# A recurrent block with a routed feed-forward beside it: the f2 stage of an item moved into the following step

## The reference

```
xn = layernorm(x)
for l in 0..3:                                    # branch 1, each item apart
    k, q, v = split(h @ Wkqv[l])
    r = tril(q k^T)/sqrt(128) / (1 + sqrt(row));  r = r / clip(|row sum|, 1);  u = r v
    a, g = split(u @ Wm1 + bm1);  m = a * silu(g) @ Wm2 + bm2
    y = groupnorm1(m) + h                         # mean and variance over the whole item
    f = gelu(y @ Wf1 + bf1) @ Wf2 + bf2
    h = layernorm(f + y) * ln_g + ln_b
e = argmax(softmax(xn @ gate_w))                  # branch 2, one of 8 experts a token
t = prob_e * (gelu(xn @ w1[e] + b1[e]) @ w2[e] + b2[e])
out = x + h * silu(t)
```

## Time and profile before

| | |
|---|---|
| median of 3 runs | 515.69 us (514.87 to 517.4) |
| the profiled execution, its own time | 514.47 us |
| its span, first to last instruction | 512.4 us |
| PE, DVE, ACT, POOL busy | 93%, 75%, 50%, 49% |
| granted TensorE clock, mean | 0.97 |

### The profile page before, as it was taken

The page is one execution under the profiler, slowest core; times in us unless marked ns, Lnnn a source line. Parts: engine busy times, 40 slices in busy tenths (PEclk is TensorE's granted clock), DMA queues, the critical chain, the costliest instruction groups (busy, mean ns, idle before and its releaser), DMA issues.

```text
span 512.4 us, 9849 instructions
## 1 busy us (share of the span) xinstructions
PE 475.0 (93%) x3147; PEld 395.4 (77%) x3147; DVE 384.8 (75%) x1348; ACT 253.7 (50%) x533; POOL 252.5 (49%) x279
## 2 busy tenths in 40 slices
PE   6999889999999999999999999999999999997472
PEld 5887666667888988898889888988888888675242
DVE  4768888878777786677777866777778777888766
ACT  4822434444566655555666555556665544453420
POOL 4520288887545445554454455544444555333341
PEclk9998999999999999999999999999999999999856
DMA  9999411112511111110111111201111000500202
GB/s 265 232 122 222 156 37 38 37 33 78 103 64 58 42 58 42 59 63 32 59 57 44 58 51 48 65 31 59 62 51 46 10 12 12 164 1 1 61 19 84
DMA packets 47345, 35.05 MB, mean 68 GB/s; under 512 B 13320, under 2 KB 38736, under 8 KB 47296
## 3 DMA queue, kind: packets, MB, share of 16 engines
q1 hardware_dynamic: 44496, 28.94, 22.1%
q0 software_dynamic: 2272, 4.71, 2.7%
q10 hardware_dynamic: 528, 0.79, 0.5%
HBM read 14.70 MB, written 9.42 MB: 47 GB/s over the span
## 4 chain that ended last, share of the span: by engine, by line
PE 67%; DVE 12%; POOL 10%; issue 6%; DMA 2%; ACT 2%; POOLq 0%; SPq 0%; DVEq 0%; ACTq 0%
PE bank L1221 9%; PE bank L1148 7%; PE bank L1132 7%; POOL x_slots L471 5%; PE pair L1290 4%; PE pair L1266 4%; PE bank L1303 4%; PE bank L1159 4%; PE pair L1248 4%; PE bank L1160 4%; PE bank L1161 3%; PE pair L1292 3%; PE pair L1246 3%; PE bank L1203 2%; PE bank L1219 2%
## 5 line engine op out<-in xcount | busy, mean ns | idle before, releaser
L483 POOL TENSOR_TENSOR zhat<-zhat,all_lg 128x512 f32<-128x512 f32 x31 | 43.9, 1418 | 88.1 <-PE bank L1193 74.2
L1221 PE MATMUL bank<-all_f,G_sb 128*128 128x128 f32 x512 | 76.8, 284 | 0.0
L651 ACT ACTIVATE y_sb<-bank,gn_bi,gn_sc 128x512 f32<-128x512 f32 x32 | 24.9, 778 | 104.3 <-DVE gn_bi L993 104.2
L1221 PEld LDWEIGHTS bank<-all_f,G_sb 128*128 128x128 f32 x512 | 70.9, 201 | 1.4 <-issue 1.4
L646 ACT ACTIVATE uT_h<-bank 128x512 fp32r<-128x512 f32 x32 | 19.1, 597 | 100.8 <-PE bank L1203 100.8
L426 POOL TENSOR_TENSOR ln_rs<-ln_ve,half_neg 128x4 f32<-128x4 f32 x32 | 33.1, 1033 | 42.0 <-DVE ln_ve L675 41.7
L1132 PEld LDWEIGHTS bank<-moe_w,h_T 128*128 128x128 f32 x312 | 39.5, 191 | 13.9 <-issue 13.9
L498 POOL TENSOR_TENSOR gn_rs<-gn_ve,half_neg 128x1 f32<-128x1 f32 x32 | 18.5, 577 | 58.5 <-DVE gn_ve L888 58.4
L563 ACT ACTIVATE h_T<-bank,w_t 128x128 f32<-128x128 f32 x156 | 44.5, 372 | 5.1 <-PE bank L1148 5.1
L518 POOL DMA_INDIRECT y_rows<-yt,slot_info x39 | 40.9, 1048 | 11.0 <-POOL yt L515 11.0
L631 ACT ACTIVATE G_sb<-bank,all_par 128x512 f32<-128x512 f32 x64 | 43.1, 694 | 5.2 <-PE bank L1184 2.8
(11 more groups left out here) (177 smaller groups left out, 1233.8 us busy)
## 6 DMA issues: line engine op xcount, KB each, us to landing
w_t<-moe_w SPq DMA_DIRECT2D x39, 258.0 KB, 2.4
x_slots<-moe_w SPq DMA_DIRECT2D x1, 2515.5 KB, 20.4
xt<-x_slots SPq DMA_DIRECT2D x39, 64.0 KB, 1.8
x_sb<-in_L_attn_x SPq DMA_DIRECT2D x8, 256.0 KB, 5.7
moe_w<-in_L_ffn_w SPq DMA_DIRECT2D x1, 2048.0 KB, 20.0
moe_w<-y_rows SPq DMA_DIRECT2D x8, 256.0 KB, 4.6
out<-moe_w SPq DMA_DIRECT2D x7, 256.0 KB, 2.4
all_f<-in_L_attn_Wf SPq DMA_DIRECT2D x2, 512.0 KB, 4.2
```

The costliest lines, as they stand in the source:

```text
L483: pool.tensor_tensor(zhat[:, b % 2, :, :], zhat[:, b % 2, :, :], all_lg[:, li, :].unsqueeze(1).broadcast_to([P, C, D]), ALU.mult)\
L1221: last = mm(bank[7][:, at_c], G_sb[:, k, at_c], all_f2[:, li, k, :], start=False, stop=k == 1)
```

## The change

**What moves.** z and its statistics, the moments, the power, ln_nb and zhat of an item leave stage 2 and become the front of stage 3 of the following step. On PE z stands right behind q; the transposition of zhat goes to the rear, ahead of u's transposition and `means`. POOL's two htok instructions wait for zhat and write htok directly, no longer in place. The groupnorm affine and y (DVE, ACT) leave the rear of a step for the front of the next. y_sb has two buffers, since z reads y one step later. On DVE the causal mask goes behind the two products on gg_sb. On POOL `ln_pow` goes behind the first place of scatters, htok behind the second, and gn's power behind htok and the LATE tile's rows. In step 7 three f1 splits stand ahead of gn's power (before: two ahead, one behind). All 24 steps of layers 1 to 3 are parted. tanh, silu and outputs come later and in other portions.

**GpSimd in the routed steps of layer 0**, before, from one item's htok (steps 4 and 5): x_slots rows are scatters, gn_rs and ln_rs the two powers.

The core of the diff:

```diff
-        y_sb = sb("y_sb", [P, S])
+        y_sb = sb("y_sb", [P, 2, S])
         def parted(l, t):
-            return turn(l, t, EARLY) is not None and l > 0
+            return 0 < l < L
-        TANH_AT = {LB - 2: (0, 1, 2), LB - 1: (3, 4, 5), LB: (6, 7)}
-        SILU_AT = {LB - 2: (0, 1, 2), LB - 1: (3, 4, 5), LB: (6, 7)}
-        OUT_AT = {LB - 1: (0, 1, 2), LB: (3,), LB + 1: (4, 5)}
+        TANH_AT = {LB - 2: (0, 1), LB - 1: (2, 3), LB: (4, 5), LB + 1: (6, 7)}
+        SILU_AT = {LB - 2: (0, 1), LB - 1: (2, 3), LB: (4, 5), LB + 1: (6, 7)}
+        OUT_AT = {LB - 1: (0,), LB: (1, 2), LB + 1: (3, 4, 5)}
@@ gpsimd step
+                scatter(l, t, 0)
+                if w := at(l, t, 3, B, LB):
+                    ln_pow(w[0], w[1])
+                tile_rows(l, t, EARLY)
+                scatter(l, t, 1)
                 w = at(l, t, 3, B, LB)
...
-                    if n < LAST_LAYER:
-                        pool.wait_ge(pe_zT, n + 1)
-                    else:
-                        pool.wait_ge(z_done, n + 1)
-                    pool.tensor_tensor(zhat[:, b % 2, :, :], zhat[:, b % 2, :, :],
+                    pool.wait_ge(z_done, n + 1)
+                    pool.tensor_tensor(rows_b, zhat[:, b % 2, :, :],
...
                 tile_rows(l, t, LATE)
                 if w := at(l, t, 1, B, LB):
                     pool.wait_ge(gn_var, w[0] + 1)
...
-                scatter(l, t, 1)
-                if w := at(l, t, 2, B, LB):
-                    ln_pow(w[0], w[1])
@@ scalar step
+                tile_gelu(late_turn_before(l, t))
+                if w := at(l, t, 2, B, LB):
+                    n = w[0]
+                    act.wait_ge(gn_affine, n + 1)
+                    act.activation(y_sb[:, n % 2, :], bank[6][:, :], ACT.Identity, bias=gn_bi[:, :],
+                                   scale=gn_sc[:, :]).then_inc(gn_done, 1)
+                queries(l, t)
...
+                gate(l, t)
...
+                layernorm(l, t)
                 tile_gelu(turn(l, t, EARLY))
@@ tensor step
+                gelu_second(l, t)
...
-                if not first:
-                    tile_front(l, t, EARLY, n2 * 2)
-                if parted(l, t):
-                    zhat_by_feature(l, t)
+                tile_front(l, t, EARLY, n2 * 2)
...
-                for stage in ((gelu_second, means, u_by_feature) if first and 2 <= t < B - 1 else
-                              (means, gelu_second) if l == L else (u_by_feature, gelu_second, means)):
-                    stage(l, t)
+                zhat_by_feature(l, t)
+                u_by_feature(l, t)
+                means(l, t)
```

More of the change, by code:

```diff
@@ L589, in late_turn_before @@
             def late_turn_before(l, t):
[L591 removed]
+                if l * B + t == 0:
                     return None
@@ L930, in step @@
                                              ALU.add, ALU.mult).then_inc(act_done, 1)
+                if w := at(l, t, 0, B, LB):
+                    n, b, _ = w
+                    dve.wait_ge(pe_A, n + 1)
+                    dve.tensor_tensor(A_sb[:, :, :], pair[:, 0, :].rearrange("p (c i) -> p c i", c=C),
+                                      causal[:, :].unsqueeze(1).broadcast_to([P, C, P]), ALU.mult)\
+                        .then_inc(A_done, 1)
+                tile_in(l, t, EARLY)
+                if s == LB + 2:
+                    outputs((LAST_B - 1,))
+                if w := at(l, t, 3, B, LB):
+                    n, b, _ = w
+                    ln_shifts(n, b)
+                    need(dve, htok_done, n - 1)
+                    dve.wait_ge(ln_shift, n + 1)
+                    for c in range(C // 2):
+                        last = dve.tensor_scalar(zhat[:, b % 2, c, :], bank[7][:, c * D:(c + 1) * D],
+                                                 ln_rs[:, b % 2, c:c + 1], ln_nb[:, b % 2, c:c + 1], ALU.mult, ALU.add)
+                    last.then_inc(z_half, 1)
+                if s == LB + 2:
+                    finish_last()
                 if first and t == 1:
```

152 lines of the change are left out of this document (49 added, 103 removed).

## The result

The changed kernel takes 561.9 us (560.4 to 564.1, 4 runs) against 515.3 for the kernel before (513.4 to 517.4, 4 runs): ratio 1.091, 95% interval 1.085 to 1.097. The direction was forecast, the size was not: 543 us, range 526 to 555. The profiled execution has a span of 559.1 us against 512.4.

A forecast was written before the change was run, and what follows sets the result against it. TensorE was taken to set the pace from step 8 to 28, GpSimd in layer 0's routed steps. Terms 7.1 + 4.7 + 1.5 + 2.9 + 6.3 + 5.1 + 0.9 - 1 = 27.5 raised 514.5 to 542, median 543 us; range 526 to 555.

The forecast's parts named there:

- two-turn steps: Sixteen steps with two expert tiles (9 to 14, 16 to 21, 23 to 26): 15.25 us against 14.80, 7.0 us in all.
- some 0.2: Two-turn steps: TensorE's idle time, once ahead of f1's second half and once ahead of `means`.
- The round was closed through GpSimd alone: Two-turn steps: gs to gn_sc runs through the LATE yt, GpSimd's weighing, indirect DMA and gn's power, 3.13 us.
- One-turn steps: Steps 8, 15 and 22, with one expert tile: 14.73 us against 13.17, 4.7 us in all.
- The collision with htok: VectorE's gs with two SBUF inputs waits beside GpSimd's htok: 0.6 us more in a one-turn step.
- f1 in parts: f1 in three parts saves TensorE some 0.3 us in six steps where it isn't last: counted as nothing.
- Layer 0: Routed steps: steps 4 to 6 at 15.3 us against 13.27, 6.3 us in all; steps 1 to 3 add 5.1.
- Six scatters: Layer 0: they stand between gn's power and ln_rs on GpSimd, 7.7 us with the gap, while VectorE stands still.
- steps 1 to 3: Start of layer 0: a later mask, and step 2's power at some 64.2 instead of 60.6; 5.1 us.
- Steps 28 to 30: Step 28, same chain as one-turn steps with an EARLY yt: 1.5 us; tile-less steps 29 and 30: 2.6 together.
- The end: Step 32 onward: VectorE's queue adds up to 39.5 to 41 us against 40.98, so -1 us (-3.5 to 0.5).
- the second (557 us): Rival, 14%: two-turn steps collide too, as ln_rs stops gg or htok reaches gs; 0.8 x 17 = 14 us.

The follow-up runs named there:

- e1_loads: Changed kernel with TensorE's two register loads moved to the rear of the step before, ahead of zhat's transposition: 552.3 us, ratio 1.072.
- e11_double: Kernel before the change with TensorE's two register loads at the start of each step made twice: 532.1 us, ratio 1.031.
- e14_behind4: Kernel before the change with TensorE's register loads made twice and placed behind the Wm2 product: 525.8 us, ratio 1.019.
- e9_ahead: Changed kernel with VectorE's xtT of the EARLY tile ahead of the mask and TensorE's register loads right behind the Wm2 product: 544.5 us, ratio 1.053.
- e5_xtT: As e1_loads on the changed kernel, with VectorE's copy xtT of the EARLY tile also put ahead of the mask: 552.0 us, ratio 1.068.
- e4_gs: Changed kernel with gs's last two instructions as tensor_scalar with one tensor input instead of two in SBUF: 559.6 us, ratio 1.087.
- e8_f1: Kernel before the change with only f1 split in three parts in every step of layers 1 to 3: 526.5 us, ratio 1.018.
- e10_f1: Changed kernel with f1 in parts only in steps with an EARLY tile, as before the change: 560.0 us, ratio 1.082.
- e6_both: Changed kernel with four scatters instead of six ahead of ln_rs in layer 0, and gs without two SBUF inputs: 554.0 us, ratio 1.070.

## Why the prediction was wrong in size

**The step that failed** is the two-turn steps: "3.13 + 6.96 + 0.35 + 2.26 + 2.55 = 15.25 us, against 14.80 for TensorE's work", 7.0 us in all, where 21.9 were measured. By the same links the trace of after has 3.16 + 7.73 + 0.43 + 2.33 + 2.55 = 16.20: four hold to 0.1 us, and the second, from gn_sc to xtT, is 7.73 for 6.96, of which VectorE stands 0.71 ahead of yt. What failed:

- The idle times of TensorE were taken as "some 0.2" twice, as if the rest of TensorE's queue stayed as it was. Each new wait took more than its own length. TensorE's queue stood in the wait for gs and had lost its lead over the engine when it came to the register loads: 0.56 us in step 19 (e1_loads takes 0.46 a step off, 7.3 us in sixteen; e11_double and e14_behind4: the same four loads cost 0.67 or 0.24 us a step). I had not priced the loads at all. They stand in no row that I had read, since the timeline leaves them out and they were covered; the trace of before has them, 1.3 us a pair.
- The round was closed through GpSimd alone. It closes through TensorE too: yt waits for the EARLY back, and so all that TensorE loses ahead of it comes back in xtT. That is why the losses add up to 16.2 and are not swallowed in 15.25. With the wait for xtT and the loads' exposure gone, a step takes 15.15 (e9_ahead). With the loads in a place where they are still exposed, taking the wait away changed nothing (e5_xtT).

**One-turn steps**: 5.1 for 4.7, but not all by the reasons given. From gn_sc to the mask there are 6.15 us for 6.16, as forecast (253.95 and 260.10 in the trace). The collision with htok cost 0.13 us (gs's L973 took 0.29, not 0.16) and not 0.6, in step 15 as in 29 and 30, and e4_gs gained nothing there. e1_loads and e9_ahead give 0.5 for step 15: exposed loads stood in the collision's place. So the term is right in part by luck.

**f1 in parts** was forecast at nothing since TensorE isn't last in those steps. In the kernel before it costs 9 us (e8_f1). In the changed kernel y_h and y_l were in my chain, so the sum holds, but the reason was incomplete: in e10_f1, where they are gone, VectorE waits for z next, which stands ahead of the gate products on TensorE.

**Layer 0** is right in size, and e6_both shows that the two mechanisms together are the cause in steps 4 to 6. The prediction's two prices were not right: it put the collision at 1.2 of 2.1 us a step, and alone it is worth nothing in steps 4 to 6. In the changed kernel gs takes 1.2 us beside htok in steps 3 and 5 only; in 4 and 6 its first such instruction is held 0.1, since gs comes as htok ends. Six scatters and the collision cover each other. In steps 1 to 3 the two are worth 3.3 of the 5.6 us; gn's power of step 2 comes at 63.76, where 64.2 was forecast (60.56 before). The round between gn powers is 15.41 us for 15.3:

```profile
79.47 0.57 POOL L495 TENSOR_TENSOR gn_rs<-gn_ve,half_neg 128x1 f32<-128x1 f32 x1 [1.73 <-DVE gn_ve L872]
...
87.99 1.05 POOL L422 TENSOR_TENSOR ln_rs<-ln_ve,half_neg 128x4 f32<-128x4 f32 x1
...
94.88 0.57 POOL L495 TENSOR_TENSOR gn_rs<-gn_ve,half_neg 128x1 f32<-128x1 f32 x1 [1.43 <-DVE gn_ve L872]
```

**Steps 28 to 30** took 3.7 for 4.1, shifted by one: in 29 gn's power still waits for the last LATE tile's DMA, which ends at 476.34, 0.03 us ahead of the power. **The end** took 1.8 more for 0.7 less. Before, TensorE stalled 5.08, 1.46 and 2.91 us there (for y, gs, y), 9.5 in all; now it stalls 2.60, 3.45, 1.87 and 3.65 us (for gg, gs, y, G_sb), 11.6 in all, and my adding up of VectorE's queue did not see that. Of the stall for gs a run shows a part: two gs instructions take 1.15 and 1.22 us beside htok, and without that (e4_gs, e6_both) the end takes 55.2 and 55.3 us, for 56.2 to 56.4 in the changed kernel and in five others with its end. Beyond that no run shows the reason, and 1.8 us are no more than this stretch varies by where the code is that of the kernel before. In e11_double and e14_behind4, with that code from step 31 on, it takes 56.9 and 56.7 us for 54.5. GpSimd's first htok instruction starts there beside three of VectorE's with two SBUF inputs. In the kernel before it took 2.61 us and VectorE's next ones their 0.68 to 0.75; in e11_double it took 1.40, and VectorE's 1.75 twice, so that gg came 2.1 us later. The first row is of the kernel before, the other two of e11_double:

```profile
480.58 2.61 POOL L483 TENSOR_TENSOR zhat<-zhat,all_lg 128x512 f32<-128x512 f32 x1 [1.95 <-ACT zhat L585]
...
495.28 1.40 POOL L483 TENSOR_TENSOR zhat<-zhat,all_lg 128x512 f32<-128x512 f32 x1 [1.95 <-ACT zhat L585]
...
497.16 1.75 DVE L919 SCALAR_TENSOR_TENSOR gg_sb<-th_sb,gg_sb 128x512 f32<-128x512 f32 x1
```

TensorE's waits in the changed kernel:

```profile
522.59 1.95 PE L1161 MATMUL bank<-y_sb,all_f 128*128 128x512 f32 x4 [2.60 <-ACT gg_sb L568]
...
529.46 0.59 PE L1208 MATMUL bank<-gs,mean_of 128*128 128x2 f32 x2 [3.45 <-DVE gs L976]
...
541.91 0.45 PE L1196 MATMUL bank<-ident,y_sb 128*128 128x128 f32 x1 [3.65 <-ACT G_sb L623]
```

**The rivals**: the second (557 us) came nearest in size, by another cause. ln_rs did not stop gg in two-turn steps: VectorE's gg keeps its 0.68 us where it starts inside the power.

## What to carry to other kernels

A wait added to an engine that was busy throughout can cost more than the time it waits: price what its queue does next, since register loads and the like, which the timeline leaves out, come out from under the work that was handed over. Ask the profile for them by their line, and read how long before the engine runs dry they are through. Close a chain through every engine that it touches, and look at which engine's wait ends last at each hand-over, before summing the links. And where two causes hold the same step, undoing one can show next to nothing: undo both before calling either free.
